# w_proj's weighted column sums with w_proj as the stationary operand, and the engines' orders laid out anew

## What is computed

```python
xn = _layernorm(x)
out = x + attention(xn, Wq, Wk, Wv, Wo) + ffn(xn, W_fc, ln_w, ln_b, W_proj)
# ffn:
h = gelu(einsum('btd,hd->bth', x, absmean(W_fc)), approximate=False)
h = (h - mu) * rsqrt(var + eps) * ln_w + ln_b
return einsum('bth,dh->btd', h, absmean(W_proj))
```

## Time and profile before

| | |
|---|---|
| Median of 3 runs | 398.52 us (396.35 to 399.64) |
| The profiled execution's own time | 397.85 us |
| Its span, first to last instruction | 396.0 us |
| PE / DVE / ACT / POOL busy | 373.7 / 321.2 / 287.6 / 231.4 us |
| HBM traffic | 29 GB/s over the span |

### The profile page before, as it was taken

The page is one execution under the profiler, slowest core; times in us unless marked ns, Lnnn a source line. Parts: engine busy times, 40 slices in busy tenths (PEclk is TensorE's granted clock), DMA queues, the critical chain, the costliest instruction groups (busy, mean ns, idle before and its releaser), DMA issues.

```text
span 396.0 us, 13503 instructions
## 1 busy us (share of the span) xinstructions
PE 373.7 (94%) x5820; PEld 268.1 (68%) x5820; DVE 321.2 (81%) x645; ACT 287.6 (73%) x329; POOL 231.4 (58%) x186
## 2 busy tenths in 40 slices
PE   0698898999999999999999999999999999999995
PEld 0346565776577776876677775876677775778873
DVE  3898878699869998699959898599968898998555
ACT  2764249887986698767986698777977598768871
POOL 7901023866586548655576548655576647769871
PEclk9999989999999999999999999999999999999999
DMA  7459009600940267021910258021930256002002
GB/s 272 153 78 123 2 10 181 87 19 5 165 51 18 48 125 134 2 65 33 198 30 18 48 116 142 4 63 33 190 38 17 52 97 109 2 17 66 30 29 82
DMA packets 30685, 29.22 MB, mean 74 GB/s; under 512 B 5665, under 2 KB 29281, under 8 KB 30625
## 3 DMA queue, kind: packets, MB, share of 16 engines
q1 hardware_dynamic: 30624, 28.35, 36.6%
HBM read 7.35 MB, written 4.19 MB: 29 GB/s over the span
## 4 chain that ended last, share of the span: by engine, by line
PE 85%; DMA 4%; DVE 4%; ACT 3%; SPq 2%; issue 1%; POOL 1%; POOLq 1%; ACTq 0%
PE small L1600 15%; PE big L1539 13%; PE big L1513 11%; PE small L1611 10%; PE big L1590 7%; PE big L1578 5%; PE big L1553 5%; PE big L1525 5%; PE small L1627 5%; PE big L1583 4%; PE big L1559 4%; DMA mask_k<-mask_k 2%; SPq L374 2%; DMA gel<-in_w_fc 2%; PE small L1617 2%; PE big L1501 2%
## 5 line engine op out<-in xcount | busy, mean ns | idle before, releaser
L578 POOL TENSOR_TENSOR p_parts<-probs,p_parts 128x1024 f16<-128x1024 f32 x64 | 136.2, 2132 | 112.8 <-ACT p_parts L762 112.8
L761 ACT ACTIVATE probs<-big,exp_scale 128x1024 f32<-128x1024 f32 x64 | 71.4, 1116 | 22.9 <-PE big L1583 20.7
L1016 DVE TENSOR_REDUCE negmax<-big 128x8 f32<-128x1024 f32 x64 | 77.6, 1222 | 7.1 <-PE big L1559 5.7
L762 ACT ACTIVATE p_parts<-big,exp_scale 128x1024 f16<-128x1024 f32 x64 | 71.3, 1115 | 0.0
L1600 PE MATMUL small<-proj_t,g_hi 128*128 128x256 f16 x256 | 57.7, 273 | 0.0
L1600 PE MATMUL small<-proj_t,g_lo 128*128 128x256 f16 x256 | 57.5, 273 | 0.0
L776 ACT ACTIVATE g_hi<-big,lnw_s 128x512 f16<-128x512 f32 x64 | 39.8, 690 | 17.2 <-PE big L1590 17.2
L1539 PE MATMUL big<-fc_t,xt_hi 128*128 128x512 f16 x128 | 48.5, 379 | 1.0 <-DVE g_lo L1010 1.0
L1539 PE MATMUL big<-fc_t,xt_lo 128*128 128x512 f16 x128 | 48.6, 379 | 0.0
L1010 DVE SCALAR_TENSOR_TENSOR g_lo<-big,lnw_s,g_hi 128x512 f16<-128x512 f32 x64 | 46.5, 746 | 2.2 <-ACT g_hi L776 1.8
L749 ACT ACTIVATE gel<-big 128x1024 f32<-128x1024 f32 x32 | 32.7, 1025 | 12.6 <-PE big L1539 12.2
(11 more groups left out here) (130 smaller groups left out, 812.2 us busy)
## 6 DMA issues: line engine op xcount, KB each, us to landing
q_stack<-qk_split SPq DMA_DIRECT2D x48, 128.0 KB, 4.0
k_stack<-qk_split SPq DMA_DIRECT2D x48, 128.0 KB, 5.3
x_in<-in_x SPq DMA_DIRECT2D x8, 512.0 KB, 5.5
out<-y_bufs SPq DMA_DIRECT2D x32, 128.0 KB, 2.4
v_odd<-v_even SPq DMA_DIRECT2D x16, 132.0 KB, 2.5
v_odd<-v_even SPq DMA_DIRECT2D x16, 99.0 KB, 2.2
gel<-in_w_fc SPq DMA_DIRECT2D x1, 1024.0 KB, 6.7
y_bufs<-in_w_proj SPq DMA_DIRECT2D x1, 1024.0 KB, 8.8
```

The costliest lines, as they stand in the source:

```text
L578: g.tensor_tensor(p_lo[:, (b * NJ + j) % PB], probs[:, (b * NJ + j) % PB], p_hi[:, (b * NJ + j) % PB], ALU.subtract).then_inc(*sig(p_lo_re ...
L761: s.activation(probs[:, (b * NJ + j) % PB].rearrange("p i (u q) -> p u i q", u=2), st, ACT.Exp, scale=exp_scale[:, 0:1]).then_inc(*sig(exp ...
L762: s.activation(p_hi[:, (b * NJ + j) % PB].rearrange("p i (u q) -> p u i q", u=2), st, ACT.Exp, scale=exp_scale[:, 0:1]).then_inc(*sig(p_hi ...
L1016: v.tensor_reduce(negmax[:, :, j], slot[b, "sa", j][:].rearrange("p a (u k) -> p (a u) k", k=P), AX.X, ALU.max, negate=True).then_inc(*sig ...
```

## The change

1. crow: proj_t is now the stationary operand, in 16 blocks of 128x128 (2 halves of the 256 output features, 8 blocks of hidden features), and six columns move (three parts of ln_w and of ln_b). The result has the output features on the partitions, 6 columns for each half.
2. `copy_row`: DVE adds the three parts (a reduction to 128x4) and multiplies the identity by each of the four columns, which gives diagonal matrices in `mean_term` (a buffer that is free at that time). csum multiplies a full matrix of ones by them, two fp32 products of 256 columns, which puts each sum on all partitions. `copy_sums` is as before.
3. The lists of all five engines are written anew. In the start, crow goes from before sa 0 to behind sa 3, v comes before fc 2, `copy_masks` before the stacks, `shift_values` behind `load_maxima`; ACT's `normalize(1)` goes behind `gelu(0, 3)`; DVE does `copy_row` behind the split maxima. In the period, wo 1 and wo 2 stand between qk 1 and gt 2, pv 6 and ct 0 before st 0, ct 1 behind mt, and many sa, st, pv and proj steps change places. The repeated part of PE's list is run three times, not twice, with `FIRST` and `LAST` shorter.

The diff, cut to its core (the rest are moves of the same kind in the lists of PE's end, SP, POOL, ACT and DVE):

```diff
@@ -84,7 +84,7 @@
         ntheta = sb("ntheta", [P, 2], fp32)
         exp_scale = sb("exp_scale", [P, 1], fp32)
         attn_scale = sb("attn_scale", [P, 1], fp32)
-        crow = sb("crow", [1, 2 * D], fp32)
+        ccol = sb("ccol", [P, KD, 2], fp32)
         csum = sb("csum", [P, 2, D], fp32)
 
         ident = sb("ident", [P, P], fp32)
@@ -263,56 +263,50 @@
-        FIRST = [(0, "wmax", 0), (0, "spread", 0), (0, "sums", 0), (0, "wmax", 1), (0, "xt", 0), (0, "spread", 1),
-                 (0, "qk", 0), (0, "sums", 1), (0, "qk", 1), (0, "fc", 0), (0, "fc", 1), (0, "fc", 2), (0, "v", 0),
-                 (0, "crow", 0), (0, "sa", 0), (0, "sa", 1), (0, "fc", 3), (0, "sa", 2), (0, "sa", 3), (0, "sa", 4),
-                 (1, "xt", 0), (0, "sa", 5), (0, "sa", 6), (0, "csum", 0), (0, "sa", 7), (0, "gt", 0), (1, "qk", 0),
-                 (0, "mt", 0), (0, "gt", 1), (1, "qk", 1), (0, "gt", 2), (0, "gt", 3), (0, "st", 0), (1, "fc", 0),
-                 (0, "proj", 0), (1, "fc", 1), (1, "fc", 2), (1, "fc", 3), (0, "st", 1), (1, "v", 0), (0, "proj", 1),
-                 (0, "st", 2), (1, "sa", 0), (0, "pv", 0), (0, "pv", 1), (0, "st", 3), (1, "sa", 1), (1, "sa", 2),
-                 (0, "proj", 2), (1, "sa", 3), (0, "st", 4), (0, "pv", 2), (1, "sa", 4), (0, "pv", 3), (1, "sa", 5),
-                 (2, "xt", 0), (0, "st", 5), (0, "proj", 3), (1, "sa", 6), (1, "sa", 7), (1, "gt", 0), (2, "qk", 0),
-                 (1, "gt", 2), (1, "gt", 3), (0, "pv", 6), (0, "ct", 0), (1, "st", 0), (2, "fc", 0), (2, "fc", 1),
-                 (2, "fc", 2), (2, "fc", 3), (0, "pv", 7), (1, "st", 1), (2, "v", 0), (1, "proj", 0), (1, "st", 2),
...
+        FIRST = [(0, "wmax", 0), (0, "spread", 0), (0, "sums", 0), (0, "xt", 0), (0, "wmax", 1), (0, "spread", 1),
+                 (0, "qk", 0), (0, "qk", 1), (0, "sums", 1), (0, "fc", 0), (0, "fc", 1), (0, "v", 0), (0, "fc", 2),
+                 (0, "sa", 0), (0, "sa", 1), (0, "fc", 3), (0, "sa", 2), (0, "sa", 3), (0, "crow", 0), (0, "sa", 4),
+                 (0, "sa", 5), (1, "xt", 0), (0, "sa", 6), (0, "sa", 7), (0, "gt", 0), (1, "qk", 0), (0, "mt", 0),
+                 (0, "gt", 1), (1, "qk", 1), (0, "gt", 2), (0, "csum", 0), (0, "gt", 3), (0, "st", 0), (1, "fc", 0),
+                 (1, "fc", 1), (1, "fc", 2), (1, "fc", 3), (0, "st", 1), (1, "v", 0), (0, "pv", 0), (0, "proj", 0),
+                 (0, "st", 2), (1, "sa", 0), (0, "proj", 1), (1, "sa", 1), (1, "sa", 2), (0, "st", 3), (0, "pv", 1),
+                 (1, "sa", 3), (0, "proj", 2), (1, "sa", 4), (0, "st", 4), (0, "pv", 2), (1, "sa", 5), (2, "xt", 0),
+                 (0, "pv", 3), (0, "st", 5), (1, "sa", 6), (0, "proj", 3), (1, "sa", 7), (1, "gt", 0), (2, "qk", 0),
+                 (0, "pv", 6), (1, "gt", 2), (1, "gt", 3), (0, "ct", 0), (1, "st", 0), (0, "pv", 7), (2, "fc", 0),
+                 (2, "fc", 1), (2, "fc", 2), (2, "fc", 3), (1, "st", 1), (2, "v", 0), (1, "proj", 0), (1, "st", 2),
...
-        PERIOD = [(3, "st", 0), (2, "pv", 6), (4, "fc", 0), (2, "ct", 0), (4, "fc", 1), (4, "fc", 2), (4, "fc", 3),
-                  (2, "pv", 7), (3, "st", 1), (4, "v", 0), (3, "proj", 0), (3, "st", 2), (3, "proj", 1), (4, "sa", 0),
-                  (3, "pv", 0), (3, "st", 3), (4, "sa", 1), (4, "sa", 2), (3, "pv", 1), (3, "proj", 2), (4, "sa", 3),
-                  (3, "st", 4), (2, "wo", 0), (4, "sa", 4), (3, "pv", 2), (4, "sa", 5), (5, "xt", 0), (3, "st", 5),
-                  (3, "proj", 3), (2, "ct", 1), (4, "sa", 6), (4, "sa", 7), (4, "gt", 0), (3, "pv", 3), (5, "qk", 0),
-                  (4, "mt", 0), (3, "st", 6), (3, "pv", 4), (4, "gt", 1), (3, "pv", 5), (3, "st", 7), (5, "qk", 1),
-                  (2, "wo", 1), (4, "gt", 2), (4, "gt", 3), (2, "wo", 2), (2, "wo", 3)]
-        LAST = [(5, "st", 0), (4, "pv", 6), (6, "fc", 0), (4, "ct", 0), (6, "fc", 1), (6, "fc", 2), (6, "fc", 3),
-                (4, "pv", 7), (5, "st", 1), (6, "v", 0), (5, "proj", 0), (5, "st", 2), (5, "proj", 1), (6, "sa", 0),
...
+        PERIOD = [(2, "st", 3), (3, "sa", 3), (2, "pv", 1), (2, "proj", 2), (3, "sa", 4), (2, "st", 4), (1, "wo", 0),
+                  (3, "sa", 5), (4, "xt", 0), (2, "pv", 2), (2, "st", 5), (3, "sa", 6), (2, "proj", 3), (2, "pv", 3),
+                  (3, "sa", 7), (3, "gt", 0), (4, "qk", 0), (3, "mt", 0), (1, "ct", 1), (2, "st", 6), (2, "pv", 4),
+                  (3, "gt", 1), (2, "st", 7), (2, "pv", 5), (4, "qk", 1), (1, "wo", 1), (1, "wo", 2), (3, "gt", 2),
+                  (3, "gt", 3), (2, "pv", 6), (2, "ct", 0), (3, "st", 0), (4, "fc", 0), (4, "fc", 1), (1, "wo", 3),
+                  (4, "fc", 2), (4, "fc", 3), (2, "pv", 7), (3, "st", 1), (4, "v", 0), (3, "proj", 0), (3, "st", 2),
+                  (4, "sa", 0), (3, "proj", 1), (4, "sa", 1), (4, "sa", 2), (3, "pv", 0)]
+        LAST = [(5, "st", 3), (6, "sa", 3), (5, "pv", 1), (5, "proj", 2), (6, "sa", 4), (5, "st", 4), (4, "wo", 0),
...
-        ORDER = FIRST + [(p + ahead, kind, n) for p in range(2) for ahead, kind, n in PERIOD if p + ahead < NB] + LAST
+        ORDER = FIRST + [(p + ahead, kind, n) for p in range(3) for ahead, kind, n in PERIOD if p + ahead < NB] + LAST
@@ -418,82 +412,82 @@
             load_norm()
             load_ffn(1)
             load_x(1)
+            copy_masks()
             load_stack(0, 0, 0)
             load_stack(0, 0, 1)
             load_stack(0, 1, 0)
             load_stack(0, 1, 1)
-            copy_masks()
+            load_maxima(0)
             shift_values(0, 0)
-            load_maxima(0)
+            shift_values(0, 1)
             load_stack(1, 0, 0)
+            load_stack(1, 0, 1)
             load_x(2)
-            shift_values(0, 1)
-            load_stack(1, 0, 1)
             load_stack(1, 1, 0)
             load_stack(1, 1, 1)
             shift_values(1, 0)
             shift_values(1, 1)
             load_maxima(1)
             load_stack(2, 0, 0)
+            load_stack(2, 0, 1)
...
@@ -799,10 +780,10 @@
             qk_upper(0, 1)
             gelu(0, 0)
             gelu(0, 1)
+            v_upper(0)
             gelu(0, 2)
-            v_upper(0)
+            gelu(0, 3)
             normalize(1)
-            gelu(0, 3)
             xt_upper(1)
             gelu_upper(0, 0)
             gelu_upper(0, 1)
...
@@ -1149,7 +1157,13 @@
 
             def copy_row():
                 dve.wait_ge(*at(0, crow_done, 1))
-                v.tensor_copy(crow[:], slot[0, "crow", 0][0:1, :]).then_inc(*sig(crow_copied))
+                link_pre(v.tensor_reduce(ccol[:], slot[0, "crow", 0][:, 0:6 * KD].rearrange("p (h a c) -> p h c a", h=KD, c=2),
+                                         AX.X, ALU.add))
+
+                for c in range(2):
+                    for h in range(KD):
+                        last = v.tensor_scalar(mean_term[:, c, h * P:(h + 1) * P], ident[:], ccol[:, h, c:c + 1], None, ALU.mult)
+                last.then_inc(*sig(crow_copied))
 
             def copy_sums():
                 dve.wait_ge(*at(0, csum_done, 1))
@@ -1158,9 +1172,9 @@
             statistics(0)
             weight_maxima(0)
             largest(0)
-            weight_maxima(1)
             scales(0)
             thresholds(0)
+            weight_maxima(1)
             weight_lower(0)
             largest(1)
             xt_lower(0)
@@ -1168,293 +1182,293 @@
             scales(1)
             qk_lower(0, 0)
             thresholds(1)
+            split_norm()
+            qk_lower(0, 1)
             weight_lower(1)
-            qk_lower(0, 1)
-            split_norm()
             ternary(1)
-            hidden_statistics(0, 0)
             statistics(1)
             v_lower(0)
-            hidden_statistics(0, 1)
-            copy_row()
+            hidden_statistics(0, 0)
             maximum(0, 0)
             maximum(0, 1)
             maximum(0, 2)
             maximum(0, 3)
             maximum(0, 4)
+            maximum(0, 5)
             xt_lower(1)
-            maximum(0, 5)
             maximum(0, 6)
             maximum(0, 7)
             gelu_lower(0, 0)
             gelu_lower(0, 1)
             split_maxima(0)
-            copy_sums()
+            copy_row()
             qk_lower(1, 0)
             gelu_lower(0, 2)
             gelu_lower(0, 3)
             qk_lower(1, 1)
             gelu_lower(0, 4)
             gelu_lower(0, 5)
+            copy_sums()
             gelu_lower(0, 6)
             gelu_lower(0, 7)
+            hidden_statistics(0, 1)
             hidden_statistics(0, 2)
             hidden_statistics(0, 3)
             hidden_statistics(1, 0)
+            hidden_statistics(1, 1)
+            hidden_statistics(1, 2)
             statistics(2)
-            hidden_statistics(1, 1)
...
+                gelu_lower(p + 3, 0)
+                gelu_lower(p + 3, 1)
+                split_maxima(p + 3)
+                qk_lower(p + 4, 0)
+                context_lower(p + 1, 1)
+                scale_context(p + 2, 4)
+                scale_context(p + 2, 5)
```

(19 more changed lines are left out.)

379 lines of the change are left out of this document (191 added, 188 removed), and 51 rows, old and new, of tables (FIRST, LAST).

## The result

The changed kernel takes **413.1 us** (median of 4 runs, 411.5 to 414.3) against 398.2 (396.4 to 399.6): a ratio of 1.037, interval 1.031 to 1.043, so 15 us slower. The forecast was 399.2, with a range of 396.0 to 402.0. The profiled execution took 413.9, its span is 412.1.

The account below looks back on a forecast made before the run. PE was taken to bound the kernel, busy 94% of the span. Terms -1.6 + 2.0 - 0.6 + 0.3 + 0.9 = +1.0 us on the profiled 397.85 gave 398.85, carried partway to the median as 399.2; range 396.0 to 402.0.

Parts of the forecast that it names:

- The middle and the tail: Repeated period and last batch: every wait of PE met in time, closest fc 0 by 0.3 us; both cost nothing.
- Its +0.3: Batch 1: proj 0 no longer between fc 0 and fc 1, so fc 3 waits for the first gelu; +0.3 us.
- Masks first, -1.6: Start: mask DMAs issued ahead of the stacks, so sa 0 waits for the stacks alone, at 38.4; -1.6 us.
- The pause, +2.0: Ahead of sa 0: PE idle 5.4 us, clock at half for about 4.4; +2.0 us, bounds 0 and 3.
- The step behind it, -0.6: From sa 0 to the last g_hi: 21.2 us for 21.8, if the later half-clock stretch stays away; -0.6 us.
- The support that I took from the opening: Sign for the pause's clock fall: opening products took 0.40 us each, later ones 0.17, after an almost idle opening.
- Crow: Column sums: 16 pairs take 0.5 us; removing the old 5.1 us, inside a wait, is worth nothing by itself.
- csum: Spread of the column sums: same columns as before, so the same 1.1 us.
- Switches, +0.9: PE's tile-shape changes between full array and tiled sa or st steps: 221 for 212, 0.1 us each; +0.9 us.
- Rival 3: Each period: fc 0 of the next batch stalls for DVE's g_lo, 0.5 us a batch; +3.5, 402.7 us; 11%.

Follow-up runs that it names:

- experiment 1: Changed kernel with the next batch's q stack copies ahead of the two stores of wo 1 and wo 2 (batches 3 to 7): 404.0 us, ratio 1.014.
- experiment 3: Changed kernel with sa 0 behind proj 1 again in every batch, SP's list untouched: 403.7 us, ratio 1.014.
- experiment 5: Changed kernel with q copies ahead of the stores, and batch 1's eight stack copies ahead of the v shifts and the load of x(2): 404.9 us, ratio 1.016.
- experiment 8: Changed kernel with q copies ahead of the stores, sa 0 behind proj 1, and batch 1's stack copies ahead of the v shifts: 406.8 us, ratio 1.021.
- experiment 10: Changed kernel with q copies ahead of the stores and SP's list of batch 1 as in the kernel before: 405.8 us, ratio 1.020.
- experiment 14: Changed kernel with q copies ahead of the stores, and in batch 1 the q copies also ahead of the v shifts: 401.7 us, ratio 1.011.
- experiment 13: Changed kernel with q copies ahead of the stores, crow moved ahead of sa 0 behind the old 48 products as filler: 400.2 us, ratio 1.006.
- experiment 15: Changed kernel with q copies ahead of the stores, the old 48 products as filler, and batch 1's q copies ahead of the v shifts: 399.7 us, ratio 1.006.
- experiment 4: Kernel before with only the new crow, copy_row and csum, in the old place ahead of sa 0: 400.4 us, ratio 1.006.
- experiment 7: Kernel before with the new column sums ahead of sa 0 and the masks first, all orders kept: 398.4 us, ratio 1.001.
- experiment 12: Kernel before with new column sums and masks first, plus the old 48 products as filler, their result overwritten: 396.3 us, ratio 0.997.

## Why the prediction was wrong, by its own steps

**The failed step is "The middle and the tail ... every wait of PE is met in time ... Both nothing."** I had walked PE, DVE, ACT and POOL through a period, but not SP's list and the landings, although the change moved two stores ahead of the q copies. In its place the runs showed a wait of sa 0 for its last k copy in each of batches 3 to 7, 1.0 to 2.1 us. The walk should have had one more line, which the trace of the kernel before could have priced: `store(b, 2)` needs wo 2, wo 2 stands behind qk 1, so the first of twelve copies goes out some 5 us later; twelve copies take 15.8 us from the first issue to the last landing; sa 0 was 6.9 us clear of that and moved 1.85 forward: 6.9 - 4.6 - 1.85 leaves 0.4. The copies took 1.5 longer as well (17.3 for 15.8), which makes the stall of 1.2 us of batch 4; why they did is open. For batch 7, with 3.75 clear, the same sum without that gives a stall of 2.7, and 2.1 was measured, with copies that took 0.9 less than before. Experiments 1 and 3 show both halves. It cost 9.0 us in the six intervals, of which 1.2 stay when the copies are put first.

**Batch 1** failed for the same reason, SP's list not walked. Its +0.3 was for fc 3 behind the first gelu, and that came (0.4). But it cost 5.1 from fc 0 to gt 0: sa 0 waited 2.6 us for its copy, and the clock fell again behind that for 3.4 us, half of which, 1.7, is lost; 0.4 remain. The second v shift moved ahead of the stacks, and csum, which x(2) waits for by way of POOL, behind gt 2. None of the four lists tried in experiments 5, 8, 10 and 14 serves all: stacks first makes pv 0 and x(2) wait, x(2) early waits for POOL, and the best, experiment 14, leaves a wait of 0.6.

**Masks first, -1.6**: -1.25 from qk 0 to sa 0, -1.27 when done alone. But I gave the fall of the clock at 49 in the earlier trace rows to the gappy score stretch. With the masks alone that stretch has the same gap of 0.5 us ahead of sa 6 and the pause of 1.9 us at 38 is gone, and so is the fall, and a second 1.25 us (forecast at 1.5, in the next step) with it. So the pause has to do with it, though not alone, since some executions of the kernel before, none of them profiled, show no fall by their mean clock. One moved line was worth 2.9 us by the medians, 1.1 against the executions without the fall.

**The pause, +2.0**: right in mechanism, too large in size. The fall is there, at 37 to 44 us. Against the 20.96 us from sa 0 to fc 0 of batch 1 at full clock and in the changed order (experiments 13 and 15) it cost 1.4, and against the 20.86 of the old order 1.9 and 2.7 in experiments 4 and 7, within my bounds of 0 and 3. The step behind it, -0.6, came to -1.15, so that the stretch cost +0.3 where +1.4 was forecast. The support that I took from the opening was misread: 0.40 against 0.17 us divides stretches by all their instructions, two one-column products among them; the products of 512 columns repeat every 0.43 and then 0.215 us, which says the same. Here the Trainium skill, page "TensorE: Matmul & The Clock Gate", section "HAM oscillation — how this bites in real kernels", was against the change, and experiments 4, 7 and 12 agree with it: behind idle stretches of 7.7 and 6.2 us the clock was at 0.50, with 0.8 in their place at 1.00.

**Crow**: 16 pairs in 0.51 us by their starts, 0.5 forecast; csum 1.0 us, 1.1 forecast. That taking out 5.1 us of work gives nothing was right, and too kind: the work was what kept the clock (experiment 12).

**Switches, +0.9**: the period with no wait in it is 44.95 us against 44.74, 1.2 in the six intervals; it fits in size. But the count is not of what the sentence says: 212 and 221 are all changes of the tile's shape, with sa, st and mt each a shape of its own. Between the full array and sa or st there are 186 and 178, fewer after the change, which would have made the term -0.8. The traces of the kernel before and of experiment 1 favour the first count: a proj step takes 1.76 us ahead of a full-array step and 1.84 ahead of sa or st, and an sa step 0.47 ahead of another sa and 0.57 ahead of anything else, st included. By that sum a period is 0.1 longer, and 0.2 was measured; the rest is open. The last batch's +1.0 I had at nothing; 0.7 of it are waits of PE (3.0 us in sum for 2.3), the largest new one 0.5 at pv 7 of batch 6.

**The start, +1.9**: 1.1 is w_fc landing at 10.06 in place of 8.95. In the nine other kernels profiled with that opening qk 0 starts at 17.1 to 18.1 (17.3 in the kernel before), so most of it belongs to this one execution and not to the change. The two spans differ by 16.1 us, the medians by 14.9.

**Rival 3** came nearest. It had the kind of thing, a stall in each period, and 3.5 us of its price, at 11%, but the place and the cause wrong (fc 0, by DVE). My range was too narrow because the transfers were in neither the walk nor the bounds.

## What to carry to other kernels

Walk the queue that issues the transfers like an engine: for each transfer, what is ahead of it in the list, when that may go, and how far the landing is from its consumer. A store that waits for a late result, put ahead of a copy, delays the copy, and every transfer behind it, by that wait; it costs what is left of the delay when the margin of the nearest consumer is used up. And before taking work out of a wait, look what the granted clock does in the emptied stretch: here 5.1 us of work in a wait was worth 2 to 3 us.
